# Cross-attention on one Trainium2 core: the transposed probabilities held stationary and 17 value columns per head streamed, in place of a small stationary value matrix and 128 streamed token columns

## The reference: what is computed

```
q = _split_heads(x @ qw + qb)          # 16 heads of 16 features
k = _split_heads(ctx @ kw + kb)
v = _split_heads(ctx @ vw + vb)
scores = jnp.einsum('bqhd,bkhd->bhqk', q, k) / np.sqrt(D // H).astype(np.float32)
probs = jax.nn.softmax(scores, axis=-1)
out = jnp.einsum('bhqk,bkhd->bqhd', probs, v)
...
ca = _mha(input_tensor, ctx_tensor, ctx_attn_mask, cq_w, cq_b, ck_w, ck_b, cv_w, cv_b)
x = _self_output(ca, input_tensor, co_w, co_b, co_g, co_be)
```

## Time and profile before

| | |
|---|---|
| median of 3 runs | 1106.69 us (1104.7 to 1110.28) |
| the profiled execution's own time | 1105.0 us |
| its span in the trace | 1103.3 us, 20772 instructions |
| TensorE matmul busy | 1019.7 us (92%) |
| TensorE weight load busy | 603.6 us (55%) |
| VectorE busy | 785.4 us (71%) |
| ScalarE busy | 608.7 us (55%) |
| GpSimd busy | 330.6 us (30%) |

### The profile page before, as it was taken

One profiled execution on the slowest core, in us unless ns is written; L12 is line 12 of the kernel. 1 busy time (PEld: TensorE's weight loads), 2 busy tenths in 40 slices (PEclk: granted clock), 3 DMA queues, 4 the chain that ended last, 5 costly groups with the idle time before them and its releaser, 6 DMA issues.

```text
span 1103.3 us, 20772 instructions
## 1 busy us (share of the span) xinstructions
PE 1019.7 (92%) x7648; PEld 603.6 (55%) x7648; DVE 785.4 (71%) x1337; ACT 608.7 (55%) x1191; POOL 330.6 (30%) x724
## 2 busy tenths in 40 slices
PE   5999989999999999999988899859898999999997
PEld 3676666433333333333344665628787777576764
DVE  5787577679999999999632855716545759787565
ACT  2665654478888888888843214112232456556543
POOL 4431111001010434344012533543365536420010
PEclk9999999889999999999998997969999999999999
DMA  7302222431221222212143100010354311000000
GB/s 211 70 16 87 93 67 95 173 122 43 77 72 47 72 60 62 71 50 69 42 134 119 38 6 15 34 62 16 103 179 130 101 49 49 20 30 1 21 15 25
DMA packets 97578, 75.67 MB, mean 69 GB/s; under 512 B 49806, under 2 KB 87483, under 8 KB 97223
## 3 DMA queue, kind: packets, MB, share of 16 engines
q1 hardware_dynamic: 94407, 65.95, 19.7%
q0 software_dynamic: 3072, 8.39, 2.3%
HBM read 42.94 MB, written 30.93 MB: 67 GB/s over the span
## 4 chain that ended last, share of the span: by engine, by line
PE 73%; DVE 8%; DMA 6%; ACT 4%; SPq 4%; POOL 3%; issue 3%; DVEq 0%; POOLq 0%; ACTq 0%
PE TR L853 16%; PE OUT L853 16%; PE OUT L1088 11%; PE TR L859 9%; PE TR L1077 9%; DMA head_q<-MT 4%; PE OUT L1077 4%; PE TR L929 3%; SPq L649 2%; PE SCR L913 2%; ACT PTS L1296 2%; PE SCR L906 2%; DVE small L1484 1%; PE OUT L859 1%; PE SCR L960 1%
## 5 line engine op out<-in xcount | busy, mean ns | idle before, releaser
L1553 DVE TENSOR_REDUCE small<-SCR 128x1 f32<-128x1024 f32 x256 | 308.5, 1223 | 28.1 <-PE SCR L960 22.0
L1394 ACT ACTIVATE shared<-TR 128x512 f32<-128x512 f32 x352 | 200.1, 597 | 40.0 <-PE TR L1077 31.6
L960 PE MATMUL SCR<-head_k,head_q 48*128 48x512 f32 x512 | 195.3, 459 | 2.7 <-DVE P L1529 2.7
L1088 PE MATMUL OUT<-shared,HM 128*32 128x256 f32 x2048 | 166.9, 398 | 1.2 <-ACT shared L1394 0.4
L1077 PE MATMUL TR<-head_q,head_k 51*128 51x512 f32 x352 | 150.7, 466 | 0.9 <-issue 0.6
L1917 POOL TENSOR_SCALAR small<-small 128x1 f32<-128x1 f32 x112 | 27.6, 247 | 355.4 <-DVE small L1485 353.3
L853 PE MATMUL TR<-xT,fifo 128*128 128x512 f32 x224 | 107.1, 636 | 1.5 <-ACT xT L1274 1.5
L1394 ACT ACTIVATE shared<-OUT 128x512 f32<-128x512 f32 x160 | 95.8, 599 | 18.6 <-PE OUT L1077 16.5
L1077 PEld LDWEIGHTS TR<-head_q,head_k 51*128 51x128 f32 x352 | 61.0, 188 | 77.4 <-ACT shared L1394 57.7
L1088 PEld LDWEIGHTS OUT<-shared,HM 128*32 128x32 f32 x2048 | 41.5, 108 | 94.4 <-ACT shared L1394 57.9
L1296 ACT ACTIVATE PTS<-TR 96x512 f32<-96x512 f32 x128 | 69.2, 589 | 42.9 <-PE TR L859 42.6
(11 more groups left out here) (241 smaller groups left out, 1867.1 us busy)
## 6 DMA issues: line engine op xcount, KB each, us to landing
pieces<-pieces SPq DMA_DIRECT2D x16, 512.0 KB, 2.7
HM<-dispatched SPq DMA_DIRECT2D x46, 128.0 KB
expert_out<-HM SPq DMA_DIRECT2D x46, 128.0 KB
dispatched<-HB SPq DMA_DIRECT2D x6, 768.0 KB, 4.0
head_q<-pieces SPq DMA_DIRECT2D x32, 128.0 KB
head_k<-pieces SPq DMA_DIRECT2D x32, 128.0 KB
shared<-in_L_ffn_w SPq DMA_DIRECT2D x4, 1024.0 KB, 11.9
x<-TOK SPq DMA_DIRECT2D x16, 128.0 KB, 1.7
```

The costliest lines, as they stand in the source:

```text
L960: ins = nc.tensor.matmul(SQ[kt % 2][:, hf, :], QX[n % 2][rows, kt * 128:(kt + 1) * 128], KX[n % 2][rows, hf * 512:(hf + 1) * 512], start=T ...
L1088: ins = nc.tensor.matmul(PV[32 * g:32 * g + 32, 0:256], VH[:, n % 2, kt, :], PTB[:, kt % 2, g * 256:(g + 1) * 256], start=(kt == 0), stop= ...
L1394: nc.scalar.activation(PTB[:, kt % 2, hf * 512:(hf + 1) * 512], ring_bank("t_scores", n, kt, hf), ACT.Exp, scale=DH ** -0.5).then_inc(st_d ...
L1553: nc.vector.tensor_reduce(nm[:, n % 2, kt:kt + 1], SQ[kt % 2].rearrange("p h n -> p (h n)"), AX, ALU.max, negate=True).then_inc(sq_done.se ...
```

## The change

`PV` is turned round. `PTS` of a head (96 keys by 128 tokens) becomes the stationary operand, and the head's 17 value columns (16 and the ones) are the moving operand, read straight from `VS0` or `VS1`. The result has tokens on partitions at once, at columns `h * 17` of an `OUT` bank. So `OT` with its four transposes, the copy to `OSB` on ScalarE, the buffer `VSW` and its two copies per layer go away, and the VectorE work that stood at `OT` stands at `PV` and reads its bank in steps of 17 instead of 32. `CA` gets two buffers, and the tables lose the `OT` words; all other words keep their order.

```diff
     "T": dict(tr=4),
-    "PV": dict(tr=1),
-    "OT": dict(out=1),
+    "PV": dict(out=1),
...
 def attention_order(before, tiles):
     for t in tiles[:-1]:
-        for a, b in (("PV", "T"), ("OT", "PV"), ("CT", "OT"), ("PJ", "CT")):
+        for a, b in (("PV", "T"), ("PJ", "CT")):
             before((a, t), (b, t + 1))
         if t + 2 in tiles:
             before(("T", t), ("S", t + 2))
+            before(("CT", t), ("PV", t + 2))
             before(("LT", t), ("PN", t + 2))
...
-        VSW = sb("VSW", [128, H, 32])
...
-        CA = sb("CA", [128, D])
+        CA = sb("CA", [128, 2, D])
...
                     def values(t):
                         self.copied("T", t)
+                        bank = out_bank(tl)
+                        for h in range(H):
+                            place = h % 8 // 2 * 4 + h // 8 * 2 + h % 2
+                            ins = nc.tensor.matmul(bank[:, h * VW:(h + 1) * VW], PTS[0:KP, place, :],
+                                                   small_values[0:KP, t // TB, h, :], start=True, stop=True)
+                        ins.then_inc(out_full.sem, 1)
+
+                    def ca_transposes(t):
+                        pe.wait_ge(out_done.sem, tl.after(out_done, "PV", t))
                         bank = tr_bank(tl)
-                        for h in range(H):
-                            g, c = h % 4, h // 4
-                            place = h % 8 // 2 * 4 + h // 8 * 2 + h % 2
-                            ins = nc.tensor.matmul(bank[32 * g:32 * g + 32, c * 128:(c + 1) * 128], VSW[0:KP, h, :],
-                                                   PTS[0:KP, place, :], start=True, stop=True)
-                        ins.then_inc(tr_full.sem, 1)
-
-                    def out_transposes(t):
-                        self.copied("PV", t)
-                        bank = out_bank(tl)
-                        transposes(bank, [OSB[:, c * 128:(c + 1) * 128] for c in range(4)]).then_inc(out_full.sem, 1)
-
-                    def ca_transposes(t):
-                        pe.wait_ge(out_done.sem, tl.after(out_done, "OT", t))
-                        bank = tr_bank(tl)
-                        transposes(bank, [CA[:, k * 128:(k + 1) * 128] for k in range(KD)]).then_inc(tr_full.sem, 1)
+                        transposes(bank, [CA[:, t % 2, k * 128:(k + 1) * 128] for k in range(KD)]).then_inc(tr_full.sem, 1)
...
-                def values(t):
-                    bank = emptied(tl)
-                    nc.scalar.activation(OSB[:, :], bank, ACT.Copy).then_inc(tr_done.sem, 1)
...
                 def normalise(t):
-                    bank = filled(tl).rearrange("p (h d) -> p h d", d=32)
+                    bank = filled(tl)[:, 0:H * VW].rearrange("p (h d) -> p h d", d=VW)
                     chain(nc.vector.reciprocal(rsum, bank[:, :, DH]))
-                    signal_out(tl, nc.vector.tensor_tensor(CA[:, :].rearrange("p (h d) -> p h d", d=DH),
+                    signal_out(tl, nc.vector.tensor_tensor(CA[:, t % 2, :].rearrange("p (h d) -> p h d", d=DH),
...
-                return {"S": scores, "OT": normalise}
+                return {"S": scores, "PV": normalise}
...
-                nc.vector.tensor_copy(KBW[:, 0:small_keys.shape[1]], small_keys)
-                nc.vector.tensor_copy(VSW[0:KP, :, 0:VW], small_values).then_inc(vsw_ready.sem, 1)
+                nc.vector.tensor_copy(KBW[:, 0:small_keys.shape[1]], small_keys).then_inc(vsw_ready.sem, 1)
```

More of the change, by code:

```diff
@@ L142 @@
+SV.14 QK.3 MX.1.5 MX.1.6 FL MX.1.7 SV.15
 """
@@ L179 @@
+LT.11 S.15 T.14 E.15 FP.7 PN.10 CT.12 PV.14 FP.6 T.15 PJ.12 LT.10 PN.12 CT.13 FC.2 PV.15 PJ.13 CT.14 RX.15 PJ.14 PN.13
+LT.12 PN.14 CT.15 FP.8 LT.13 PJ.15 LT.14 PN.15 FP.9 FP.10 LT.15 FP.11 FC.3 FP.13 FP.15 FP.12 FP.14
 """
@@ L223, in schedule_a @@
             before(("S", t - TB), ("VW", 1))
-            before(("PV", t - TB), ("VW", 1))
             before(("S", t), ("MX", 0, 0))
@@ L559, in build @@
         resid_ready = Signal(sem("residual_ready"), **count("res"))
-        vsw_ready = Signal(sem("small_values_ready"), **count("vsw"))
+        vsw_ready = Signal(sem("small_keys_ready"), **count("vsw"))
         pc_ready = Signal(sem("pieces_ready"), 1, **count("pc"))
@@ L889, in token_major, with attention @@
                     product(bank[:, 0:D], [(src[:, k, c:c + 128], w[:, k, :]) for k in ks]).then_inc(out_full.sem, 1)
-                def attention(self, first, nk, project):
+                def attention(self, first, nk, small_values, project):
                     tl = self.tl
@@ L947, in projected @@
                             .then_inc(out_full.sem, 1)
-                    return {"S": scores, "T": prob_transposes, "PV": values, "OT": out_transposes,
+                    return {"S": scores, "T": prob_transposes, "PV": values,
                             "CT": ca_transposes, "PJ": projected,
@@ L1044, in first_maxima @@
                     max_scores(tl0, n, kt, hf)
-            attending = at.attention(starts, SC, co)
+            attending = at.attention(starts, SC, VS0, co)
             def projected(t):
@@ L1250, in ternary_down @@
                     product(bank[:, 0:D], pairs).then_inc(out_full.sem, 1)
-                tl.walk(order_c, groups, at.attention(starts, SC1, wo) | {
+                tl.walk(order_c, groups, at.attention(starts, SC1, VS1, wo) | {
                     "ST": self_output_transposes, "SO": self_projection,
@@ L1557, in _ @@
             tl0, tl = Tally("b0"), Tally("a")
-            chain = Chain(0, links(order_a, MK=10, KB=1, LS=1, S=1, OT=1, PJ=1, PN=2))
+            chain = Chain(0, links(order_a, MK=10, KB=1, LS=1, S=1, PV=1, PJ=1, PN=2))
             waited = []
@@ L1608, in fixed_columns @@
                 nc.vector.memset(VX[:, :, :, DH:VW], 1.0)
-                nc.vector.memset(VSW[:, :, VW:32], 0.0)
                 nc.vector.memset(VH[:, :, :, VW:32], 0.0)
@@ L1714, in _ @@
             if True:
-                chain = Chain(0, links(order_c, SO=1, SN=2, FO=1, FN=5, GT=17, RK=11, CB=3, S=1, OT=1, PJ=1, FC=MF, FP=1))
+                chain = Chain(0, links(order_c, SO=1, SN=2, FO=1, FN=5, GT=17, RK=11, CB=3, S=1, PV=1, PJ=1, FC=MF, FP=1))
                 def self_norm(t):
```

47 lines of the change are left out of this document (21 added, 26 removed).

## The result

The change makes the kernel slower: 1233.49 us, median of 4 runs (1225.93 to 1235.62), against 1108.49 us for the kernel before on the same chip (4 runs, 1104.7 to 1117.62). The ratio is 1.112, with a 95% interval of 1.1068 to 1.1173. The forecast was slower, at 1210 us in a range of 1160 to 1242; the time lies in the range, 23 us above the point.

What follows compares the result with a forecast made beforehand. TensorE was taken to bound the kernel: 1105.0 us plus 63 (82.3 for new `PV`, less 14.1 for `OT`, less 5 of covered idle time) plus 42 for the falling clock gave 1210 us, range 1160 to 1242.

Steps and rivals of the forecast that it cites:

- TensorE is the bound: Both cross-attention stretches: TensorE idles only 15.5 us in all, so shorter latency from `PV` to `CT` gains nothing.
- New `PV`: Cross-attention `PV` on TensorE: 32 x 0.112 = 3.58 us a tile in place of 1.01, 82.3 us more in all.
- the first two terms: TensorE in the cross-attentions: 82.3 us more for new `PV`, 14.1 us less for the removed `OT`; 68.2 us more.
- The faster rival: `PV` loads hide beside other work: 1086 us, chance 0.05; the change wins below 45 ns per load and matmul.
- ScalarE, nothing: The `OSB` copy goes, 19.1 us of ScalarE time, but it is off the chain, so nothing is counted.
- VectorE, "Nothing": Normalisation stays two instructions, `VSW` copies go off the chain, other TensorE work precedes `CT`: no effect on time.
- First sum: 68.2 us more TensorE time, less 5 us of covered idle time: 63 us, 1105.0 to 1168 us.
- the clock holds: Rival: the clock stays up in both attention stretches, so only the first sum counts: 1168 us, chance 0.24.
- The clock, 32 x 1.7 = 54 us, less 12: The clock falls about once per `PV`, losing 1.7 us each; 12 us taken off, so 42 us more.
- the relief of 12 us: Taken off the clock's 54 us: 8.4 us of `PTS` copy waits vanish and a few groups keep the clock.
- Falls and stays down: Rival: two low-clock stretches a tile instead of one, as `PV` lasts up to 6.8 us: 1264 us, chance 0.10.
- What would show it: Profile signs: 3.6 us `PV` tiles, 190 ns loads, lower clock digits, windows some 50 us longer each, ScalarE down 19 us.

Runs made afterwards that it cites:

- round_bf16: The changed kernel with probabilities and values of `PV` rounded to bf16, one load and one matmul a product; 1095.75 us, ratio 0.9944 to the kernel before.
- stream128: The changed kernel with each `PV` matmul streaming 128 columns instead of 17, same loads; 1179.82 us, ratio 1.0639 to the kernel before.
- quarters_copy: quarters with a copy of the old `OSB`'s size put back on ScalarE at `PV`; 1133.23 us, ratio 1.0283 to the kernel before.
- quarters: The changed kernel with each `PV` load split into four column strips of 32 tokens; 1132.57 us, ratio 1.0257 to the kernel before.
- quarters_stream: quarters with 36 columns streamed in each `PV` matmul instead of 17; 1138.44 us, ratio 1.0305 to the kernel before.

## Why the prediction was right, and where its sizes were off

**TensorE is the bound, and latency from `PV` to `CT` is worth nothing.** Right for what the change removes: in the kernel after, TensorE is not waiting for `CA` in any wait that the profile lists (in round_bf16, where it has less to do, it is, for 2.6 us). Half wrong for what the change adds, below.

**New `PV`, 3.58 us a tile.** 3.50 measured, 0.109 us a load and matmul against 0.112 from the router's rows. The sum of the first two terms, 82.3 - 14.1 = 68.2 us, is to the digit the rise of TensorE's busy time in stream128, where the clock holds; so close a match is partly luck, since the low time of 8 and 9 us is open by 5. The Trainium skill, page "TensorE: Matmul & The Clock Gate", section "LDWEIGHTS (loading the stationary operand)", gives a load's time as columns / 1.2 in ns, an estimate of 107 ns for 128 columns: the trace agrees for the distance from load to load at the high clock, and differs at the low one, 205 ns (6.55 us / 32). The rule of the Trainium skill that the prediction weighed, page "TensorEngine Tiling (Array Packing)", section "Performance Considerations", 60 cycles of overhead for each matmul, gives an estimate of 25 ns at 2.4 GHz. The trace is against it by a factor of four: the rule leaves out the load, which in float32 sets the pace here.

**The faster rival, and its point of decision at 45 ns.** Excluded by the 0.109 us, and its logic was borne out: in round_bf16 the distance is 26 ns, what the earlier trace rows gave as the lower bound, with half as many products, and there the kernel is faster, if by 0.6%.

**ScalarE, nothing.** Right within what quarters_copy can tell, 3 us at its medians.

**VectorE, "Nothing".** This step was wrong in part. The normalisation on VectorE now waits for a `PV` of 3.5 us and more, and what stands behind it in VectorE's list is not only its own tile's work: the `LN0` of other tiles stands there, and TensorE has their transposes next. That is the wait for `XN` of 7.9 us in stretch A of the changed kernel and 8.1 us in stream128, against 1.2 us before. I had asked who waits for `CT` and not who waits for the rest of VectorE's queue.

**First sum, 63 us.** With the clock held it is 504.9 - 427.5 = 77.4 us in the two stretches and 73.9 in the span. The 5 us of idle time that I let the longer work cover weren't covered; idle time rose by 9.2 us instead. So the rival "the clock holds", 1168, would rather have come out near 1105.0 + 73.9 = 1179.

**The clock, 32 x 1.7 = 54 us, less 12.** The mechanism was right and is shown by stream128: few columns streamed, clock down, with TensorE busy all the while. The terms were mis-sized, with errors that cancel. The low time rose by 148 us, more than the 32 stretches of 3.4 us (109 us) that I took, since the 29 that came are 5.3 us long on average; and each us of it costs 0.40 us and not 0.5. That the product is the 54 I had, 54.5 us by the spans against stream128 and 58.1 in the two stretches, is luck. So the term that was mis-sized in the sum is the relief of 12 us: the waits for `PTS` copies did shrink, but in the two stretches only from 8.5 us to 4.8, and with 27 falls of the clock at 32 tiles few groups kept it. One of the two places in the earlier trace rows on which the mechanism rested doesn't bear it out, either: from 153.7 to 158.5 us TensorE stood idle for 2.74 of 4.80 us, so that fall is one behind a gap; only the place at 667 us has a busy TensorE that streams little. On the profiled execution 105 us were forecast, 63 and 42; 128.4 came, 73.9 and 54.5.

By the advice of the Trainium skill that the prediction weighed, page "TensorE: Matmul & The Clock Gate", section "Why this matters for your kernels", to avoid gaps, the clock would have held here. The trace is against it as the only condition: from 1028.3 to 1038.0 us TensorE never paused (busy for 9.70 of 9.70 us), and the clock fell.

**Falls and stays down, 1264.** The time lies between my case and this one. The `PV` at 215 us, 6.55 us long, is that case in the small: the clock stays low for 17.1 us around and behind it. Its own columns did not bring the clock down, though. It fell 0.3 us after this `PV` had begun, and just ahead of it TensorE had waited 2.7 us for `P`. Counted over the 32 tiles in the trace, the clock was at its low level at the start of `PV` in none: it came back each time before the next `PV` began.

**What would show it.** The group, its loads of 190 ns, its 3.5 us at the high clock and 6.55 at the low one, the digits of the clock row and ScalarE's lower load came as said (13 us lower and not 19: the copy's 19.0 us are gone, the `PTS` copies are busy for 72.5 and not 69.2 us, the rest is spread). Stretches A and C grew by 74 and 61 us, not 50 each. TensorE's idle time in them is 5.8 us larger, where I had said no larger. The rest of the kernel is 7 us shorter, not equal, by its own low time.

## What to carry to other kernels

Before swapping the operands of a product, price its loads and not only its columns: in a float32 product with 128 stationary columns each of the two loads took 0.11 us, and 17 streamed columns cost as much as 128; here that cost 2.5 us a tile to save 0.44. A TensorE group without a gap can still lose the clock, if it streams few columns; look at the granted clock behind it, and test it with added columns that nobody needs. And when an engine's wait gets longer, go through all that stands behind it in its queue, other tiles' work too.

## What the hardware did that I had not expected

- Free columns: behind a float32 load of 128 columns a matmul streams 128 columns in the time of 17 (3.59 and 3.50 us for a tile's 32), and a kernel that does this needless work is 4.3% faster (1.0639 / 1.112 = 0.957).
- Column strips load at once: two loads of 64 columns take 0.062 us (1.98 us / 32) where one of 128 takes 0.109; four of 32 take 0.038 us (1.20 us / 32).
- In runs of over a hundred loads and matmuls at some 10 ns a pair, TensorE stops with no releaser: 12 times in quarters, for up to 2.5 us, once behind 120 matmuls. The stops of over 1 us stand a multiple of 256 instructions apart, at the same numbers in quarters and in quarters_stream.
- The clock's fall costs less than half of the low time, 0.40 us for 1 us between two kernels and 0.39 us among executions of one kernel, even with TensorE busy for 93% of the span.
- Streaming 36 columns in place of 17 did no good that the runs can tell in the kernels with 32-column strips (low time 54 to 45, and 45 to 58 us, in single executions), while 64 in 64-column strips did (64 to 27). Why is open.
